# One softmax-attention block inside an eight-block kernel: its order of work around the score loop is rearranged

## The reference, cut to what matters

```python
# x: [B=2, S=1024, d=128], H=16 heads of hd=8
x_norm = layer_norm(x, g1, beta1)
q, k, v = (x_norm @ W + b for each), split into heads
q, k = apply_rope(q), apply_rope(k)
scores = einsum('bhqd,bhkd->bhqk', q / sqrt(hd), k)
attn = softmax(scores)                       # over 1024 keys
out = einsum('bhqk,bhkd->bhqd', attn, v)     # back to [B, S, d]
x = x + out @ Wo + bo
x = x + relu(layer_norm(x, g2, beta2) @ W1 + b1) @ W2 + b2     # W1: 128 x 512
```

## Time and profile before

| | |
|---|---|
| median of 3 runs (1069.44 to 1104.62) | 1072.06 us |
| the profiled execution's own time | 1078.72 us |
| its span, first to last instruction | 1076.6 us |
| granted PE clock, mean over the span | 0.813 |
| busy: PE, DVE, ACT, POOL | 769.0, 699.2, 527.6, 181.7 us |
| this block, first statistic to last add | 323.4 to 836.0 us |

### The profile page before, as it was taken

One profiled execution on the slowest core, in us unless ns is written; L12 is line 12 of the kernel. 1 busy time (PEld: TensorE's weight loads), 2 busy tenths in 40 slices (PEclk: granted clock), 3 DMA queues, 4 the chain that ended last, 5 costly groups with the idle time before them and its releaser, 6 DMA issues.

```text
span 1076.6 us, 14680 instructions
## 1 busy us (share of the span) xinstructions
PE 769.0 (71%) x5285; PEld 457.5 (42%) x5285; DVE 699.2 (65%) x1350; ACT 527.6 (49%) x1123; POOL 181.7 (17%) x177
## 2 busy tenths in 40 slices
PE   4587743599464458898888887887869559395594
PEld 2377533499342321111111111111157549385493
DVE  5844762366476967668999999996070646556363
ACT  1430441355245434457888878888524335224252
POOL 2000027345204000000000000000021345212452
PEclk9889656699776855559999999999679669797597
DMA  4820001411300000000000000000050021100213
GB/s 109 226 75 1 1 10 50 122 36 35 99 0 1 0 1 1 1 1 1 1 2 1 1 1 1 1 1 1 1 157 1 18 86 35 55 1 11 85 38 98
DMA packets 53992, 36.68 MB, mean 34 GB/s; under 512 B 9042, under 2 KB 49170, under 8 KB 53922
## 3 DMA queue, kind: packets, MB, share of 16 engines
q1 hardware_dynamic: 49154, 25.98, 8.7%
q0 software_dynamic: 4768, 9.77, 2.7%
HBM read 22.31 MB, written 13.43 MB: 33 GB/s over the span
## 4 chain that ended last, share of the span: by engine, by line
PE 49%; DVE 14%; issue 12%; ACT 11%; POOL 8%; DMA 3%; another core or an unknown queue 2%; SPq 1%; DVEq 0%; POOLq 0%; ACTq 0%
PE psum L1403 14%; PE psum L1391 10%; ACT arena L1455 7%; POOL results L937 6%; POOL slots L929 3%; PE psum L1013 3%; DVE arena L1370 2%; PE psum L236 2%; PE psum L1355 2%; PE psum L1023 2%; DVE stats L159 2%; PE psum L344 1%; PE psum L322 1%; PE psum L1521 1%
## 5 line engine op out<-in xcount | busy, mean ns | idle before, releaser
L1370 DVE TENSOR_REDUCE arena<-psum 128x2 f32<-128x1024 f32 x256 | 300.2, 1219 | 51.1 <-PE psum L1355 49.7
L1455 ACT ACTIVATE arena<-psum 128x512 f32<-128x512 f32 x512 | 264.6, 604 | 107.9 <-PE psum L1391 107.8
L1391 PE MATMUL psum<-arena 32*128 32x512 f16 x512 | 130.5, 425 | 59.7 <-ACT arena L1455 58.5
L1403 PE MATMUL psum<-arena 128*32 128x512 f32 x1024 | 156.9, 690 | 0.0
L1056 ACT ACTIVATE arena<-psum,arena 128x128 f32<-128x128 f32 x340 | 97.0, 368 | 109.1 <-PE psum L1023 61.4
L1391 PEld LDWEIGHTS psum<-arena 32*128 32x128 f16 x512 | 30.3, 93 | 247.5 <-ACT arena L1455 215.3
L1355 PE MATMUL psum<-arena 32*128 32x512 f16 x512 | 122.9, 431 | 11.7 <-DVE arena L1370 9.2
L929 POOL DMA_INDIRECT slots<-xn,arena x64 | 65.5, 1024 | 226.7 <-DVE arena L1133 208.1
L937 POOL DMA_INDIRECT results<-arena x85 | 83.6, 984 | 107.9 <-DVE arena L1215 103.6
L1013 PE MATMUL psum<-arena 128*128 128x128 f32 x680 | 97.1, 288 | 2.2 <-DVE arena L1210 2.2
L1023 PE MATMUL psum<-arena 128*128 128x128 f32 x680 | 89.5, 274 | 1.0 <-ACT arena L1056 0.7
(11 more groups left out here) (265 smaller groups left out, 1032.9 us busy)
## 6 DMA issues: line engine op xcount, KB each, us to landing
arena<-slots SPq DMA_DIRECT2D x19, 256.0 KB, 3.1
arena<-results SPq DMA_DIRECT2D x16, 256.0 KB, 4.1
slots<-blank SPq DMA_DIRECT2D x1, 2560.0 KB, 10.7
expert_w<-in_L_attn_b_w_dram SPq DMA_DIRECT2D x1, 2048.0 KB, 8.6
expert_w<-in_L_attn_b_w_dram SPq DMA_DIRECT2D x8, 256.0 KB, 4.9
expert_w<-in_L_ffn_W_dram SPq DMA_DIRECT2D x1, 2048.0 KB, 8.5
expert_w<-in_L_ffn_W_dram SPq DMA_DIRECT2D x8, 256.0 KB, 4.7
results<-arena POOLq DMA_INDIRECT x85
```

The lines of the kernel that those rows point to most:

```text
L1370: v.tensor_reduce(self.mx[:, h % 2, keys, qt, 2 * pair:2 * pair + 2], core.psum[:, 2 * slot:2 * slot + 2, :], AX.X, ALU.max).then_inc(self ...
L1391: nc.tensor.matmul(core.psum[:, 4 + tile % self.SCORE_BANKS, :], self.kT[rows, g, at:at + P], self.qT2[rows, h % 2, :], start=True, stop=T ...
L1403: last = nc.tensor.matmul(core.psum[32 * j:32 * j + 32, 7, :], self.vs[:, b * TB + kt, HG * g + j, :], self.prob[:, k % self.PROBS, j, :], ...
L1455: nc.scalar.activation(self.prob[:, k % self.PROBS, j, :], core.psum[:, 4 + tile % self.SCORE_BANKS, :], ACT.Exp).then_inc(self.prob_in, 1)
```

## The change

1. **Lead-in.** ACT now moves the first batch's tokens before it fills constants, and fills the other constants (`clear_value_pads`) after the second batch's. DVE adds the bias of q and k only; v is moved by ACT (`move_values`), and its bias, which softmax only adds, is folded into `bo` in the block before (class `ValueBias`: `bo += bv @ Wo`, one broadcast, one product, one add in cm2). DVE's order becomes bias 0, rotate 0, bias 1, split 0, rotate 1, split 1.
2. **Second batch's split transposes.** PE transposes batch 0's q and k, fills the first two ring slots, and then for each of batch 1's 8 turns issues one product that nobody reads (`keep_busy`), the 8 transposes and two ring fills. Batch 1's turns use banks 4 to 7.
3. **Products nobody reads.** Eight of them (128 x 128 by 128 x 512, fp32) also stand before batch 0's split transposes, released when DVE's high parts are written.
4. **Loop.** During halves 10 to 13 the ring has four more fills, "o": 8 transposes of `oT` for two tiles of batch 0 each, which DVE divides. In the last half, after the waves of steps 0 and 1, PE transposes batch 0's attention output, after 2 and 3 it multiplies by Wo, and after 4 and 6 it transposes four tiles of batch 1.
5. **After the loop.** Four tiles of batch 1 are left to transpose; then both batches' second halves are interleaved by hand.

The diff, cut to its core (`...` marks what is left out):

```diff
+def keep_busy(core, w, pe, bank, times):
+    for _ in range(times):
+        core.nc.tensor.matmul(core.psum[:, bank, :], w.ident[:, :], w.sa_w1[:, :], start=True, stop=True)
...
+        self.t[0]["qkT"] = core.turns(8)
+        self.t[1]["qkT"] = [core.turn_on(4 + i % 4) for i in range(8)]
...
+    def fills(self):
+        order = [("max", 0, i) for i in range(16)] + [("turn", 0, 0)] + [("max", 1, i) for i in range(16)]
+        for h in range(2, self.HALVES):
+            for i in range(16):
+                if i == 2:
+                    order.append(("turn", h - 1, 0))
+                order.append(("max", h, i))
+                if i == 8 and self.EARLY + 2 <= h < self.EARLY + 6:
+                    order.append(("o", h - self.EARLY - 2, 0))
+        return order + [("turn", self.HALVES - 1, 0)]
...
     def ring_fill(self, pe, a):
...
+        if kind == "o":
+            pe.wait_ge(self.sum_out, self.EARLY)
+            self.turn_output(pe, 2 * h, 2 * slot)
+            self.turn_output(pe, 2 * h + 1, 2 * slot + 1).then_inc(self.ring_in, 1)
+            return
...
     def loop_tensor(self, pe):
+        for i in range(4):
+            pe.wait_ge(core.emptied[i], self.before_units[i])
         a = 0
+        while a < 2:
+            self.ring_fill(pe, a)
+            a += 1
+        pe.wait_ge(self.again_in, 2)
+        pe.wait_ge(self.split_in, 2)
+        for i in range(8):
+            core.claim(pe, self.t[1]["qkT"][i])
+            keep_busy(core, self.w, pe, self.t[1]["qkT"][i].bank, 1)
+            self.turn_split(pe, 1, i)
+            self.ring_fill(pe, a)
+            self.ring_fill(pe, a + 1)
+            a += 2
...
             if k > 0:
                 self.wave(pe, k - 1)
+            if h == self.HALVES - 1:
+                if kt == 0:
+                    pe.wait_ge(self.ring_out, len(self.order))
+                if kt in (0, 1):
+                    self.turn_attention(pe, 0, kt)
+                if kt in (2, 3):
+                    self.project(pe, 0, kt - 2)
+                if kt == 4:
+                    pe.wait_ge(self.sum_out, self.HALVES - 1)
+                    self.turn_outputs_late(pe, 4)
+                if kt == 6:
+                    self.turn_outputs_late(pe, 5)
...
     def tensor(self, pe):
-        pe.wait_ge(self.pads, 5)
+        pe.wait_ge(self.pads, 3)
         pe.wait_ge(w.ident16_in, 1)
...
+        core.claim(pe, self.t[0]["qkT"][0])
+        pe.wait_ge(self.high_in, 1)
+        keep_busy(core, w, pe, self.t[0]["qkT"][0].bank, 8)
+        pe.wait_ge(self.again_in, 1)
+        pe.wait_ge(self.split_in, 1)
         for i in range(8):
+            self.turn_split(pe, 0, i)
         self.loop_tensor(pe)
         pe.wait_ge(self.sum_out, self.HALVES)
+        self.turn_outputs_late(pe, 6)
+        self.turn_outputs_late(pe, 7)
+        self.turn_second(pe, 0)
...
+        self.turn_attention(pe, 1, 0)
...
+        self.turn_attention(pe, 1, 1)
+        self.widen(pe, 0, 0)
+        self.project(pe, 1, 0)
+        self.project(pe, 1, 1)
+        self.widen(pe, 0, 1)
+        self.narrow(pe, 0, 0)
+        self.turn_second(pe, 1)
+        self.narrow(pe, 0, 1)
+        self.widen(pe, 1, 0)
+        self.widen(pe, 1, 1)
+        self.narrow(pe, 1, 0)
+        self.narrow(pe, 1, 1)
...
     def scalar(self, act):
         act.wait_ge(w.sa_in, w.sa_all)
+        deviation(core, 0)
+        deviation(core, 0, var=5, root=6)
+        for g, turn in enumerate(self.t[0]["xT"]):
+            self.move_tokens(act, turn, 0, g, 0)
+        deviation(core, 1)
+        deviation(core, 1, var=5, root=6)
+        self.clear_pads(act)
+        self.move_values(act, 0)
+        for g, turn in enumerate(self.t[1]["xT"]):
+            self.move_tokens(act, turn, 1, g, 0)
+        self.clear_value_pads(act)
+        self.move_values(act, 1)
+        self.copy_high(act, 0)
+        self.move_split(act, 0)
+        self.copy_high(act, 1)
+        self.move_split(act, 1)
         self.loop_scalar(act)
...
     def vector(self, dve):
+        self.add_bias(dve, 0)
+        self.rotate(dve, 0)
+        self.add_bias(dve, 1)
+        self.split(dve, 0)
+        self.rotate(dve, 1)
+        self.split(dve, 1)
         self.loop_vector(dve)
+        self.add_projection(dve, 0)
+        spread(core, core.xn, 0)
+        self.read_outputs_late(dve, 4)
+        self.read_outputs_late(dve, 5)
+        self.second_norm(dve, 0)
+        self.read_outputs_late(dve, 6)
+        self.read_outputs_late(dve, 7)
+        self.add_projection(dve, 1)
+        spread(core, core.xn, 1)
+        self.second_norm(dve, 1)
```

527 lines of the change are left out of this document (308 added, 219 removed).

## The result

The changed kernel took 1045.32 us in the median of six executions (1041.39 to 1123.94), the kernel before, on the same chip, 1073.12. The ratio is 0.9751, with a 95% interval of 0.9717 to 0.9785. (A few executions of either kernel come out 30 us and more above the rest, with a lower clock; the ratio leaves them out.) The forecast was 1041, the range 1015 to 1061. From median to median the change takes off 27.8 us.

A forecast was written before the change was run, and what follows sets the result against it. Bounds differed by stage: DVE's chain in the lead-in, PE in the 1.2 GHz loop, no full engine at 2.4 GHz. Terms -8.2 + 0 + 4.5 - 6.5 - 21.1 + 0.3 = -31 us, from median 1072.06 to 1041 us; range 1015 to 1061.

The forecast's parts named there:

- Lead-in: Up to the first exponential: reordered work brings it to 399.9 from 408.15; -8.2 us, between -14 and -3.
- collision with POOL: Lead-in: POOL's additions lie over DVE's rotation and make it wait; cost between 1.4 and 5.6 us, 5.6 taken.
- Loop entry: Start of the loop: the clock falls there again before the first wave, so no gain; 0 us.
- as long and as slow as before: First part of the loop at 1.2 GHz, 77.4 us in the kernel before, keeps its length and pace; 0 us.
- o fills: Loop: four added fills of 8 transposes, 1.2 us each, plus 0.9 us on DVE; +4.5 us, between 0 and 8.
- Last half: Last half of the loop: 22.2 + 4 = 26.2 us against 32.7; -6.5 us, or +8 if the clock falls.
- it holds 2.4 GHz: Last half: the added work is dense, so PE is expected to stay at the full clock; part of the -6.5 us.
- After the loop: Last sum to last add: 36.7 us against 57.8, batch 1's normalisation hidden; -21.1 us, between -24 and -16.
- The chance of "faster": Whole kernel: chance of a time below 1050.6 us, reckoned as 0.19 + 0.60 x 0.85 plus a little, 0.73.
- The clock holds at the entry: Rival, loop's entry: the clock does not fall, 76 tiles are faster; -28 us, 1013 us; chance 0.19.
- No change that can be measured: Rival: last half falls to 1.2 GHz (+14.5) and lead-in gains 3 instead of 8; 1060 us; chance 0.16.
- Slower, by a long slow part: Rival, first batch's loop: the slow part grows at 0.374 us a tile; 1108 if that whole batch is slow; chance 0.05.

The follow-up runs named there:

- Run 11: Changed kernel with only ACT's wait for constants moved behind the two roots of batch 0's normalisation; one execution, 1039.3 us.
- Run 1: Changed kernel without any of its 16 products that nobody reads; median 1055.4 us.
- run 7: Kernel before, plus one unread product ahead of each of the ring's first 25 fills (512 columns at the first turn, otherwise 256); median 1089.9 us.
- run 12: Kernel before, plus only the loop entry's unread products (one of 512 columns, eight of 256); executions of 1055.7, 1075.6, 1081.6 and 1081.9 us.
- run 4: Changed kernel plus nine unread products at the loop's entry (one of 512 columns, eight of 256); 1038.8 us, ratio 0.9685.
- run 5: Changed kernel plus three unread products of 256 columns where PE waits for ACT around the last half; 1042.7 us, ratio 0.9734.
- Run 6: Changed kernel with batch 0's output turned, projected and normalised after the loop again, without o fills; 1056.5 us, ratio 0.9877.
- run 9: Same as run 8, but with the eight products ahead of batch 0's split transposes kept; 1024.0 us, ratio 0.9549.
- run 10: Same as run 8, also without the one unread product per turn of batch 1; median 1017.9 us, ratio 0.9488.
- run 8: Changed kernel with POOL held until both splits, entry and last-half products, ACT's wait moved, no eight products ahead of batch 0; 1016.4 us, ratio 0.9496.

## Why the prediction came out right, and where not

The prediction came out right, with a total closer than its terms. The 31 us are the difference of two profiled executions, and the one before lies 5.6 us above the median of its six, the changed kernel's 2.2 us above its own. So some 3 us of what is counted below may be the choice of execution, most likely in the loop's slow part; only one execution of the kernel before has a profile.

**Lead-in (forecast -8.2, measured -7.0).** Its steps stood: tokens moved at 332.1 (331.9 forecast), second normalisation at 339.0 (338.0), collision with POOL 5.4 us (5.6), products 358.6 to 367.9 (358.0 to 367.5), ring's first read 376.6 (375.7), first exponential at 400.9 (399.9). What failed is small: the wait that the change puts ahead of ACT's roots makes the table load visible. The forecast had only asked whether the second root is late. Run 11 gives it back, 1.5 us.

**Loop entry (0, measured -13.1).** That the clock falls at the first wave was right: 400.9. The step that failed is "as long and as slow as before". It took 44.7 us instead of 77.4, and ended at the same place in five profiles. Run 1 speaks for a part of the products in it (without them 68 us in the profile, and scatter of tens of us); the other part, the pace at the second turn, is argued from runs 7 and 12. Neither is shown by itself. Both were in the diff; the forecast looked only at whether the clock falls, not at when it rises again, and had no case between 0 and -28.

**o fills (+4.5, measured +6.4).** Each costs 1.60 us and not 1.1. A half without one and a half with one, in the changed kernel:

```profile
581.40:602.40 21.00, 17.06 (x133) 3.78 (x132) 19.43 (x20) 17.02 (x34) 0.00 (x0) 1.00 0.00 1
602.40:625.00 22.60, 18.46 (x141) 4.64 (x140) 19.98 (x22) 17.03 (x34) 0.00 (x0) 1.00 0.00 1
```

DVE is busy only 0.55 us more, PE 1.40, and DVE stands idle 1.05 us more. So the larger part is not DVE's extra read but the other half of the forecast's sentence, that it meets PE at a ring of two: a reader idle while PE does the eight transposes.

**Half before the last (not seen, +1.2).** It is the new pace's later last fill, shown under run 7.

**Last half (-6.5, measured +1.8).** This is the worst term, and most of it was arithmetic. Eight waves of the earlier trace rows and 2.7 us were counted; but the stretch of the earlier trace rows holds nine such steps from wave to wave (746.70 to 774.01), with 4.4 us around them, an estimate for 2.4 GHz: at 2.4 GHz the kernel before would have needed 26.4 us there and not 22.2. So its fall had cost 6.3 us, not 10.5. The added work was put at 4 and takes 5.0 (runs 4 and 5: 29.93 us less 31.24 - 6.3 = 24.9 for the same without it and without a fall). And "it holds 2.4 GHz" was wrong by two short falls, 3.1 us (runs 4 and 5). 4.2 + 1.0 + 3.1 = 8.3, the whole miss. Run 6 speaks for the reason given all the same: without the added work the clock stayed down for the whole of that half.

**After the loop (-21.1, measured -21.9).** PE is busy 34.95 of 35.8 us, the normalisation is hidden, the clock is 1.00, as written.

**Slips that changed nothing.** The terms after the loop add up to 36.9 us, not 36.7. The last stretch of the earlier trace rows holds 40 exponentials and not 32, so that a tile at 2.4 GHz takes 260.1 / 396 = 0.657 us and not 0.644, and the rival's price is 27.6 and not 28. The chance of "faster" is reckoned with 0.85 where the sentence before it has four fifths.

**Rivals.** "The clock holds at the entry" did not come about; it takes nine more products. Its price was right: 13.1 us here and 15.5 more in run 4's profile are 28.6. "No change that can be measured" did not come about either: the last half had two short falls and not one long, and the lead-in gave 7.0. "Slower, by a long slow part" is seen in single executions: one of the changed kernel's six took 1123.94 us at clock 0.755, near the 1108 of that rival; no profile shows where its slow time lay.

## What to carry to other kernels

Where a stage's pace hangs on the clock, look for the thin places (a turn, a stage's entry, the last iterations) and fill the pauses there with a few dense products; eight standing earlier were 5.8 us of delay (run 9). Check the pace of a software ring at its first and last period: where two fills too many stood in one wave the clock fell both times (runs 7 and 12), and a last fill one wave late cost 1.2 us. Count iterations from the first and last row, not from the loop bound; and when an engine's wait is moved forward, ask what it used to do ahead of its data, a table load for one.

## What the runs showed that was not expected

- PE busy for 27.30 of 27.30 us at 1.2 GHz, and for 22.76 of the next 27.30 at 2.4 (run 7).
- Nine products, some 4 to 6 us of work at 2.4 GHz, took 15.5 us off a loop of 366 in run 4's profile, the fastest of five executions. (That of 512 columns takes 0.86; for one of 256 half of that is an estimate, and in run 10 the fill behind it starts 0.63 to 0.65 us after it.) The scatter goes with the clock: four executions within 1.5 us in run 8, within 47 in run 1.
- With work added to the last half it was shorter (33.05 us) than in the same kernel without (36.51), where the clock was down throughout; in the kernel before it took 31.24.
- A DVE reduction from PSUM is untouched by POOL beside it (2.36 us for two, with and without), where a product of two SBUF tensors goes from 1.22 to 3.37.
